# Packing the high and low columns of an expert's last gate/up chunk into full blocks

## The reference

```
x = hidden_states.reshape(-1, d)                        # 2048 x 512
scores = softmax(x @ gate_w)                            # 8 experts
topk_w, topk_idx = top_k(scores, 2)
g = silu(einsum('td,edh->teh', x, w_gate)) * einsum('td,edh->teh', x, w_up)   # h = 352
routed = einsum('teh,ehd,te->td', g, w_down, comb)      # comb: topk_w at topk_idx
shared = silu(x @ sw_gate) * (x @ sw_up) @ sw_down      # width 704
out = routed + shared
```

## Time and profile before

| | us |
|---|---|
| median of 3 runs | 730.86 (730.31 to 730.97) |
| profiled execution, own time | 730.87 |
| its span, first to last instruction | 729.1 |
| TensorE busy | 686.1 (94%) |
| TensorE weight loads busy | 565.6 (78%) |
| VectorE busy | 468.3 (64%) |
| ScalarE busy | 257.4 (35%) |
| GpSimd busy | 171.0 (23%) |

### The profile page before, as it was taken

The page is one execution under the profiler, slowest core; times in us unless marked ns, Lnnn a source line. Parts: engine busy times, 40 slices in busy tenths (PEclk is TensorE's granted clock), DMA queues, the critical chain, the costliest instruction groups (busy, mean ns, idle before and its releaser), DMA issues.

```text
span 729.1 us, 10577 instructions
## 1 busy us (share of the span) xinstructions
PE 686.1 (94%) x3796; PEld 565.6 (78%) x3796; DVE 468.3 (64%) x967; ACT 257.4 (35%) x478; POOL 171.0 (23%) x221
## 2 busy tenths in 40 slices
PE   5799999999899999997999999899999999999992
PEld 1577677778667887885887887889898998989891
DVE  3987778729899865558667635565574746566451
ACT  3445255424443324221012022444362524435130
POOL 1233133210122111000000032325434363530403
PEclk9899999999999999999999999999999999999997
DMA  9912211122345414120320424747565574853504
GB/s 306 387 55 77 74 33 40 29 85 76 101 171 180 178 73 144 58 87 1 118 78 15 141 72 130 230 97 191 95 201 67 189 122 148 186 98 63 66 0 66
DMA packets 44219, 82.52 MB, mean 113 GB/s; under 512 B 7529, under 2 KB 15721, under 8 KB 43634
## 3 DMA queue, kind: packets, MB, share of 16 engines
q1 hardware_dynamic: 35730, 62.06, 26.1%
q0 software_dynamic: 8448, 19.93, 14.4%
HBM read 59.93 MB, written 23.22 MB: 114 GB/s over the span
## 4 chain that ended last, share of the span: by engine, by line
PE 55%; DVE 12%; issue 3%; ACT 2%; DMA 2%; POOL 1%; SPq 0%; ACTq 0%; DVEq 0%; POOLq 0%
PE bank L1557 17%; PE bank L1559 17%; PE bank L1558 17%; PE bank L1808 2%; DMA sdraw<-in_L_ffn_sw_down 1%; DVE gsel L1460 1%; DVE rows L1185 1%; DVE st L991 1%; DVE u L1175 1%; ACT gsel L897 1%; DVE hx L1197 1%; DVE m L1149 1%; DVE ht L1452 1%; DVE mw L1154 1%; PE bank L1788 1%
## 5 line engine op out<-in xcount | busy, mean ns | idle before, releaser
L1557 PE MATMUL bank<-ht,ew 128*128 128x288 f32 (+1 forms) x384 | 115.4, 300 | 2.5 <-DVE bc_c L1467 1.8
L1558 PE MATMUL bank<-ht,ew 128*128 128x288 f32 (+1 forms) x384 | 113.7, 296 | 0.0
L1559 PE MATMUL bank<-ht,ew 128*128 128x288 f32 (+1 forms) x384 | 113.4, 295 | 0.0
L615 POOL DMA_INDIRECT out_rows<-y,si x40 | 61.9, 1546 | 119.2 <-DVE y L1483 107.2
L1557 PEld LDWEIGHTS bank<-ht,ew 128*128 128x128 f32 (+1 forms) x384 | 69.3, 181 | 4.1 <-DVE bc_c L1467 2.0
L1557 PE MATMUL bank<-xt,sgu 128*128 128x512 f32 x176 | 69.4, 394 | 0.8 <-DVE bc_ga L1212 0.5
L1558 PEld LDWEIGHTS bank<-ht,ew 128*128 128x128 f32 (+1 forms) x384 | 69.6, 181 | 0.3
L1559 PEld LDWEIGHTS bank<-ht,ew 128*128 128x128 f32 (+1 forms) x384 | 69.4, 181 | 0.0
L1558 PE MATMUL bank<-xt,sgu 128*128 128x512 f32 x176 | 68.6, 390 | 0.0
L1559 PE MATMUL bank<-xt,sgu 128*128 128x512 f32 x176 | 68.6, 390 | 0.0
L1557 PE MATMUL bank<-wkv,xt 128*128 128x512 f32 x128 | 55.3, 432 | 2.9 <-DVE xt L1020 2.9
(11 more groups left out here) (302 smaller groups left out, 1523.1 us busy)
## 6 DMA issues: line engine op xcount, KB each, us to landing
xring<-in_L_attn_X SPq DMA_DIRECT2D x32, 256.0 KB, 2.8
ewst<-in_L_ffn_w_gate SPq DMA_DIRECT2D x8, 704.0 KB, 5.4
ewst<-in_L_ffn_w_up SPq DMA_DIRECT2D x8, 704.0 KB, 4.4
slots<-in_L_wmod SPq DMA_DIRECT2D x4, 1024.0 KB, 6.5
x_d<-rows SPq DMA_DIRECT2D x16, 256.0 KB, 2.0
h_d<-hx SPq DMA_DIRECT2D x16, 256.0 KB, 2.0
xrow<-x_d SPq DMA_DIRECT2D x16, 256.0 KB, 2.8
out_rows<-xrow SPq DMA_DIRECT2D x16, 256.0 KB, 2.0
```

The lines of the kernel that those rows point to most:

```text
L615: pool.indirect_dma_start(out=out, out_offset=bass.IndirectOffsetOnAxis(ap=si[0:CR[j], par, j:j + 1], axis=0), in_=y[0:CR[j], j, :], in_of ...
L1557: nc.tensor.matmul(dst, a[0], b[0], start=first, stop=False)
L1558: nc.tensor.matmul(dst, a[0], b[1], start=False, stop=False)
L1559: return nc.tensor.matmul(dst, a[1], b[0], start=False, stop=last)
```

## The change

The 96-wide chunk of gate and up is packed. For each slice k of 128 rows the weights are laid out as three blocks of 128 columns instead of four of 96 (gate high, gate low, up high, up low): gate's 96 high columns with the low parts of its last 32 columns, the same for up, and a third block with the low parts of the first 64 columns of gate and of up. The first two blocks are multiplied with the tokens' high part (128 columns wide) and, their first 96 columns, with the tokens' low part; the third with the tokens' high part only, into a bank of the down stage (REST_BANKS). So each k takes five products instead of six.

The pieces lie in different partitions and banks: ScalarE copies the gate and the up bank out (`r_both_of`, a new function), VectorE adds the third block's rows to rows 0 to 63 and rows 96 to 127 to rows 64 to 95 (`summed`, new), twice, and the silu and the product then read the sums. The packed chunk now comes first in each half (M_OF), so it is chunks 0 and 3; two chunks later TensorE waits for the two copies, not for VectorE's product. The third block's products wait for the row results of the entry before (y_ready), and in the first entry for the shared rows (s_row). The high and low splits of gate and up weights are done in two pieces on ScalarE and three on VectorE, one before. Four semaphores of the wmod load are joined into one.

```diff
+WHOLE = H // P * P
+LAST = H - WHOLE
+EXTRA = P - LAST
+REST = LAST - EXTRA
+M_OF = (NR - 1,) + tuple(range(NR - 1))
...
+        REST_BANKS = DOWN_BANKS
...
             def expert_hi(w, par, q):
...
-                    nc.scalar.activation(ew[par][:, 0, lo:hi], ewst[:, slot, 0:hi - lo], ACT.Copy).then_inc(ew_hi, 1)
+                    raw = raw_columns(slot)
+                    nc.scalar.activation(whole_columns(ew[par], 0, q), raw[:, :, 0:WHOLE], ACT.Copy)
+                    nc.scalar.activation(packed_columns(ew[par])[:, :, q * P:q * P + LAST], raw[:, :, WHOLE:H], ACT.Copy)\
+                        .then_inc(ew_hi, 1)
...
+            def r_both_of(u, c):
+                act.wait_ge(gu_mm, 2 * NR * u + c + 1)
+                act.wait_ge(r_mul, 2 * NR * u + max(c - 2, 0) + 1)
+                for dst, banks in ((both_g, GATE_BANKS), (both_u, UP_BANKS)):
+                    nc.scalar.activation(dst, bank[banks[c % 2]][:, 0:HALF], ACT.Copy).then_inc(r_both, 1)
...
                     for c in range(2 * NR):
+                        if M_OF[c % NR] == NR - 1:
+                            r_both_of(u, c)
+                            if c:
+                                r_hi_of(u, par, c - 1)
                         r_silu_of(u, par, c)
...
             def expert_lo(w, par, q):
...
+                if q < 2:
+                    raw, packed = raw_columns(slot), packed_columns(ew[par])
+                    dve.tensor_tensor(whole_columns(ew[par], 1, q), raw[:, :, 0:WHOLE],
+                                      whole_columns(ew[par], 0, q).bitcast(F32), ALU.subtract)
+                    dve.tensor_tensor(packed[:, :, q * P + LAST:(q + 1) * P], raw[:, :, H - EXTRA:H],
+                                      packed[:, :, q * P + REST:q * P + LAST].bitcast(F32), ALU.subtract)
+                    last = dve.tensor_tensor(packed[:, :, 2 * P + q * REST:2 * P + (q + 1) * REST],
+                                             raw[:, :, WHOLE:WHOLE + REST],
+                                             packed[:, :, q * P:q * P + REST].bitcast(F32), ALU.subtract)
...
+            def summed(dst, both, at, par, c):
+                rest = bank[REST_BANKS[(par + c // NR) % 2]]
+                dve.tensor_tensor(dst[0:REST, 0:HALF], both[0:REST, 0:HALF], rest[at:at + REST, 0:HALF], ALU.add)
+                return dve.tensor_tensor(dst[REST:LAST, 0:HALF], both[REST:LAST, 0:HALF], both[LAST:P, 0:HALF], ALU.add)
...
+                if m == NR - 1:
+                    dve.wait_ge(r_lo, 2 * NR * u + max(c - 2, 0) + 1)
+                    dve.wait_ge(r_both, 4 * u + 2 * half + 1)
+                    summed(gbuf[c % 3], both_g, 0, par, c).then_inc(r_sum, 1)
+                    dve.wait_ge(r_both, 4 * u + 2 * half + 2)
+                    up = both_u
+                    summed(up, up, REST, par, c).then_inc(u_sum, 1)
+                    dve.wait_ge(u_sum, 2 * u + half + 1)
...
             def expert_gate_up(u, par, ahead=True):
...
-                    pe.wait_ge(r_mul, 2 * NR * u + max(c - 1, 0) + 1)
+                    if c > 1 and M_OF[c % NR - 2] == NR - 1:
+                        pe.wait_ge(r_both, 4 * u + 2 * half + 2)
+                    else:
+                        pe.wait_ge(r_mul, 2 * NR * u + max(c - 1, 0) + 1)
+                    tok = [ht[par][:, s, :, at] for s in range(2)]
+                    if m == NR - 1:
+                        packed = packed_columns(ew[par])
+                        for i, to in enumerate((GATE_BANKS, UP_BANKS)):
+                            for k in range(DC):
+                                for part in ((0, 1), (1, 0))[k > 0]:
+                                    n = r if part else P
+                                    nc.tensor.matmul(bank[to[c % 2]][0:n, 0:HALF], packed[:, k, i * P:i * P + n], tok[part][:, k, :],
+                                                     start=k == 0 and not part, stop=k == DC - 1 and not part)
+                        pe.wait_ge(s_row, NT)
+                        pe.wait_ge(y_ready, CT * u + 1)
                         for k in range(DC):
+                            last = nc.tensor.matmul(bank[REST_BANKS[(par + half) % 2]][:, 0:HALF], packed[:, k, 2 * P:3 * P],
+                                                    tok[0][:, k, :], start=k == 0, stop=k == DC - 1)
```

More of the change, by code:

```diff
@@ L271, in build @@
         bias_in, bout_in = sem("bias_in"), sem("bout_in")
-        mod_in = [sem(f"mod_in{k}") for k in range(DC)]
+        mod_in = sem("mod_in")
         x_in = [sem(f"x_in{j}") for j in range(GT)]
@@ L328, in build, with whole_columns, packed_columns, down_columns @@
         GB_AT = [(), (), (0,), (), (1, 2), (3,), (4,)]
-        EW_PART = [(0, DC * H), (DC * H, 2 * DC * H), (2 * DC * H, EW)]
+        PACKED, EW_DOWN = 4 * DC * WHOLE, 4 * DC * H
+        def whole_columns(ew, s, q):
+            at = (2 * s + q) * DC * WHOLE
+            return ew[:, at:at + DC * WHOLE].rearrange("p (k n) -> p k n", k=DC)
+        def packed_columns(ew):
+            return ew[:, PACKED:EW_DOWN].rearrange("p (k n) -> p k n", k=DC)
+        def down_columns(ew, s, r, at, n):
+            return ew[0:r, EW_DOWN + s * NR * D + at:EW_DOWN + s * NR * D + at + n]
+        def raw_columns(slot):
+            return ewst[:, slot, 0:DC * H].rearrange("p (k n) -> p k n", k=DC)
         def tile_rows(ap, t):
@@ L898, in select_gb @@
                     .then_inc(gs_ready, 1)
+            def r_both_of(u, c):
[3 more added lines that the diff above has]
+                    nc.scalar.activation(dst, bank[banks[c % 2]][:, 0:HALF], ACT.Copy).then_inc(r_both, 1)
             def r_silu_of(u, par, c):
-                half, m = divmod(c, NR)
+                half, m = c // NR, M_OF[c % NR]
                 r = RM[m]
[L903 to L906, removed]
+                gate = bank[GATE_BANKS[c % 2]][0:r, 0:HALF]
+                if m == NR - 1:
+                    act.wait_ge(r_sum, 2 * u + half + 1)
+                    gate = gbuf[c % 3][0:r, 0:HALF]
+                else:
+                    act.wait_ge(gu_mm, 2 * NR * u + c + 1)
+                    act.wait_ge(r_lo, 2 * NR * u + max(c - 2, 0) + 1)
+                nc.scalar.activation(gbuf[c % 3][0:r, 0:HALF], gate, ACT.Silu).then_inc(r_silu, 1)
             def r_hi_of(u, par, c):
-                half, m = divmod(c, NR)
+                half, m = c // NR, M_OF[c % NR]
                 r = RM[m]
@@ L1433, in expert_lo @@
             def expert_lo(w, par, q):
-                lo, hi = EW_PART[q]
                 slot = (par + q) % 2
                 dve.wait_ge(ew_hi, 3 * w + q + 1)
-                parts = [(P, lo, hi, 0)]
-                if q == 2:
+                if q < 2:
[7 more added lines that the diff above has]
+                                             packed[:, :, q * P:q * P + REST].bitcast(F32), ALU.subtract)
+                else:
                     full = H // P * D
[L1440 to L1443, removed]
+                    for r, at, n in ((P, 0, full), (RM[-1], full, D)):
+                        last = dve.tensor_tensor(down_columns(ew[par], 1, r, at, n), ewst[0:r, slot, at:at + n],
+                                                 down_columns(ew[par], 0, r, at, n).bitcast(F32), ALU.subtract)
                 last.then_inc(ew_lo, 1)
@@ L1642, in misc @@
                 elif name == "mod":
-                    for k in range(DC):
-                        pe.wait_ge(mod_in[k], 16)
+                    pe.wait_ge(mod_in, 16 * DC)
                     for k in range(DC):
@@ L1818, in expert_gate_up @@
                         pe.wait_ge(ew_lo, 3 * u + 2)
-                    pe.wait_ge(r_mul, 2 * NR * u + max(c - 1, 0) + 1)
-                    for i, to in enumerate((GATE_BANKS, UP_BANKS)):
-                        for k in range(DC):
-                            col = (i * DC + k) * H + m * P
-                            last = product3(bank[to[c % 2]][0:r, 0:HALF], [ew[par][:, s, col:col + r] for s in range(2)],
-                                            [ht[par][:, s, k, at] for s in range(2)], k == 0, k == DC - 1)
+                    if c > 1 and M_OF[c % NR - 2] == NR - 1:
+                        pe.wait_ge(r_both, 4 * u + 2 * half + 2)
+                    else:
+                        pe.wait_ge(r_mul, 2 * NR * u + max(c - 1, 0) + 1)
+                    tok = [ht[par][:, s, :, at] for s in range(2)]
+                    if m == NR - 1:
+                        packed = packed_columns(ew[par])
[7 more added lines that the diff above has]
+                        pe.wait_ge(y_ready, CT * u + 1)
+                        for k in range(DC):
+                            last = nc.tensor.matmul(bank[REST_BANKS[(par + half) % 2]][:, 0:HALF], packed[:, k, 2 * P:3 * P],
+                                                    tok[0][:, k, :], start=k == 0, stop=k == DC - 1)
+                    else:
+                        for i, to in enumerate((GATE_BANKS, UP_BANKS)):
```

(8 more changed lines are left out.)

26 lines of the change are left out of this document (14 added, 12 removed).

## The result

The changed kernel takes 729.06 us in the median of 13 runs, the kernel before, beside it, 731.13; the ratio is 0.9956 (95% interval 0.9943 to 0.9970), which is 3.2 us less (2.2 to 4.2). The forecast was 3.7 less, 727.2, with a range of 723.5 to 731.8. The executions of the kernel before lie between 729.71 and 734.33, those of the changed kernel between 727.87 and 730.35, so the comparison goes by the ratio and not by the 2.1 us between the two medians. One more execution of the changed kernel took 774.79 us at a mean granted clock of 0.837; the ratio leaves it out.

A forecast was written before the change was run, and what follows sets the result against it. TensorE, busy 94% of the span, was taken as the bound. Gains of 2.9 us in six middle experts and 1.06 in the last, less 0.25 in the first, make 3.7 off 730.87: 727.2 us, range 723.5 to 731.8.

The forecast's parts named there:

- Product spacing and width: TensorE's gate/up chunks: each 288-column product costs 0.132 us whatever the weights' width; 64 fewer save at most 8.4 us.
- weight loads set the pace: Rival on TensorE: as many weight columns are loaded as before, so no gain, 730.0 us; no-gain chance 0.16.
- Chunk 0's 0.53 whole: Middle experts' first packed chunk: no later wait takes back its saving of 0.53 us.
- Chunk 3's saving lost at the transposes of rows 2 and 3: Middle experts: TensorE waits 0.34 and 0.18 us for low halves of turned rows; 0.02 of 0.53 us remains.
- S: Start of ScalarE's activation of chunk 2 in a middle expert, the zero point of the walk; 503.03 in the trace before.
- the added work: VectorE after chunk 3: chunk 4's product late by 0 to 0.15 us, lengthening the last transposes' wait; taken as 0.06.
- Sums of 0.45, starts 0.37 apart: VectorE in packed chunks: four added sums of 0.45 us, each overlapping the next by about 0.08.
- the three held starts: VectorE: partition changes may hold three of four sums, 0.36 us per packed chunk, about 0.13 reaching TensorE; then 728.0.
- Low split 0.13 longer: VectorE's gate and up weight split in three pieces takes 1.76 us, 0.13 more, twice per expert.
- The first expert, -0.25: First expert: waits for the shared row and the longer split leave no gain and lose 0.25 us.
- mostly covered: Down weights' load: issued 1.4 us later, after chunk 0's low split, landing after 4.0 us, mostly before it is wanted.
- The last expert: Last expert: no weights or rows to prepare, so no wait takes the saving back; 1.06 us gained.

The follow-up runs named there:

- e6: Changed kernel with splits of turned rows moved ahead of output scales, and the first output row's product ahead of the last scale; ratio 0.9844 to the kernel before.
- e5: Kernel before, unpacked, with the splits of turned rows moved ahead of the output scales in chunks 2 and 4; ratio 0.9938 to the kernel before.
- e2: Changed kernel with chunk 0 given its 24 products again, chunk 3 left packed; ratio 1.0025 to the kernel before.
- e3: Changed kernel with chunk 3 given its 24 products again, chunk 0 left packed; ratio 1.0036 to the kernel before.
- e8: Changed kernel with the second sum of each pair replaced by a same-size sum starting at partition 0, result unused; ratio 0.9970 to the kernel before.
- e7: e6 with a third staging slot for the down weights, so their load no longer waits for the gate weights' low split; ratio 0.9827 to the kernel before.

## Why the prediction was right

- **Product spacing and width.** Right: a last packed expert is 1.03 us shorter for 8 products, and in e6 against e5 1.01. The packed blocks of 128 columns cost no more than those of 96. Rival "weight loads set the pace" is out.
- **Chunk 0's 0.53 whole.** Right, shown by e2.
- **Chunk 3's saving lost at the transposes of rows 2 and 3.** The wait is there, 0.35 us by the starts and a second small one inside the eight transposes (1.01 for 0.83), as worked out. The walk for the changed kernel holds: the sums begin at S + 3.25 and chunk 4 at S + 3.80, forecast 3.25 and 3.78. What each part is worth I had wrong. I gave chunk 3's saving 0.02 and the added work 0.06; by e3 (32.26 us, against 32.32 before less chunk 0's 0.53) a middle expert loses 0.47 by the added work and gains 0.41 by the earlier end of chunk 3, since VectorE's queue ends last up to the last transposes. Their sum came out right, -0.06 for -0.04, and so the expert, 0.47 for 0.49. Whoever had left chunk 3 unpacked by my 0.02 would have lost 0.4 us per middle expert.
- **Sums of 0.45, starts 0.37 apart.** The duration was right (0.43 to 0.50), the distance not: 0.45 to 0.53 in the rows above. The Trainium skill's rule (VectorE: DVE Perf Modes, section "Two Vector instructions with no wait between them") holds here: the trace has the three held starts, and in e8 two of them are gone. Chunk 4's product is late by 0.25 to 0.30 instead of my 0.06; e8 gives back 0.10 of that, and my own figures, a split of 1.83 from S + 6.05 on, would have given 0.19. But the wait before the last transposes is hardly longer, 0.34 to 0.39 for 0.33 to 0.35, since the two scales behind that product had waited for ScalarE before (from the product to rows 2 and 3 it is 2.27 us before, 2.06 after). Of the 0.13 per expert that I gave for the three held starts, e8 shows 0.04 to 0.06 for two of them.
- **Low split 0.13 longer.** Right: 1.23 + 0.29 + 0.42 with two overlaps, 1.76.
- **The first expert, -0.25.** Mis-sized: it lost 1.00. The walk of this expert stopped at the low halves of rows 0 and 1; the step that failed lies behind, "mostly covered" for the down weights' load. It is issued after chunk 0's low split, which in the first expert waits for the gate weights. Already the kernel before waits for it, 0.83 us. After, the second piece is issued 0.26 us later from chunk 0's start and lands 7.01 us after its issue instead of 6.38, so the split begins 0.88 later. The rest to 1.00 lies on VectorE between the down weights' split and the low half of row 2. Why it takes 0.63 longer to land was not tested. e7 moves the load, and with it the wait goes. I also let chunk 3 run at half clock as in the earlier trace rows; it ran at full clock, but it began 0.38 us later and TensorE waited 1.26 us before the transposes of rows 2 and 3, so chunk 4 begins no earlier than before. This term, 0.75 us off, is most of what parts the experts' 2.85 from the forecast's 3.7.
- **The last expert** had 1.03 for 1.06. **Semaphores of the load joined**: no sign of them.

What stays open: in one or two of the six middle experts of every experiment on the packed kernel, and in none of the profiled execution of the kernel after, ScalarE's first copy of chunk 3 begins 0.80 to 0.95 us after the start of the third block's last product (once 1.08, once 1.58) instead of 0.33, mostly with gaps on ScalarE and VectorE that the profile calls issue. These are the longer experts in each list above. It costs 0.2 us (e7) to 1.0 us (one expert of e8) where it appears and may be part of the spread between runs; no run was made on it.

## What to carry to other kernels

Products removed from a full TensorE are worth their spacing only up to the next wait. Walk each engine's queue from one event to the next and compare the ends; if another queue is within the saving, its order is the next thing to change, and here moving two groups of instructions gave 1.13 us per middle expert (31.85 to 30.72), where the packing alone had shown 0.47. Walk the first iteration by itself and to its end: here a load that is covered in all the others was late in it already in the kernel before. When the profiled executions differ before the changed stage begins, compare the stage, not the span.

## What the hardware showed that was not expected

Two VectorE instructions with no wait between them start 0.36 to 0.38 us apart at 288 columns when the second has its inputs and its output at partition 0 (in e8 even behind one whose PSUM input starts at partition 64), and 0.45 to 0.53, behind the end of the first, when one of its inputs starts in another 32-partition group than the last input from the same memory (SBUF or PSUM) before it (the kernel after, and the third sum of e8). A sum of two SBUF ranges that start at partitions 64 and 96 takes 0.46 us in the mean, about as long as a product of 128 partitions (0.45 to 0.46).
